# The end of a pipelined attention kernel: one DMA step, four high-part steps of ScalarE and a stretch of VectorE's order moved

## The chip, the cores and the metric

One core of one Trainium2 chip. The metric is the device time of one launch in microseconds (us); lower is better.

## What is computed

Two residual layers on x of shape (8, 1024, 512), conditioned on a vector of 256 per batch:

```python
# style = s @ aff_w.T + aff_b; every weight matrix is scaled by style per input and by rsqrt(sum of squares) per output
x = x + clip(modulated_linear(x, L0), -256, 256)
kx = modulated_linear(x, K).reshape(B, N, 16, 32)          # q = k = v = kx
scores = einsum('bnhd,bnjd->bnhj', kx, kx) / sqrt(32)      # 16 x 16 between the heads of one token
out = einsum('bnhj,bnjd->bnhd', softmax(scores), kx)
x = x + modulated_linear(out.reshape(B, N, 512), O)
```

## The kernel before, in words

All is float32 and held transposed: 512 features in four blocks of 128 partitions, tokens in the free dimension. The 8192 tokens are cut into 32 tiles of 256, numbered 0 to 31; `last` is 31. Each of the three linear layers L0, K, O takes four blocks per tile (`linear`, L446), and a block is twelve matmuls of 128x256: four input blocks by three passes. To keep float32 precision, operands are split in a high part, made by ScalarE (`hi_part`, L561: `x_hi_of`, `x1_hi_of`, `y_hi_of`), and a low part, made by VectorE (`lo_part`, L755). In the names of the trace the operand of L0 and of K is x_hi/x_lo and that of O is y_hi/y_lo. "O(29)" below is the O layer of tile 29, its four blocks.

What happens to one tile c, in order:

- L0: TensorE, evacuated from PSUM by ScalarE (`l0_out`), clipped and added to x by VectorE (`make_x1`, L839 and L841).
- K: four blocks, evacuated by ScalarE (`k_out`, trace kx<-lin_ps). The result goes to DRAM (`k_to_dram`, or block by block near the end, `k_blocks_to_dram` L263) and back in another layout (`k_from_dram` L272, four reads into k_st). VectorE turns it (`turn_k` L816, k_rhs<-k_st). This is "the turn of the keys".
- The keys are copied into a block diagonal tile k_bd, three quarters by GpSimd (`spread_k` L429), one by ScalarE (`copy_keys` L669). Then TensorE computes the scores (`scores`, L516, 64 small matmuls).
- Scores are merged from PSUM: the even ones by ScalarE (`even_scores` L633), the odd ones by VectorE (`merge_scores` L846), then maxima and subtraction (`subtract_maxima` L851, L853), the exponential on ScalarE (L655), `sums` (L865, L867), `normalise` (L871 and the transpose L877, which makes p_turned), and masks that spread the probabilities into p_bd: four on VectorE (`spread_probabilities` L884), four on ScalarE (`spread_some` L661).
- v takes its own way through DRAM: k_rhs written (`v_to_dram` L280), four reads into k_v (`v_from_dram` L288), two transposes by VectorE (`turn_v` L831).
- The product of probabilities and v (`pv`, L534, 64 small matmuls) is evacuated by ScalarE in two halves (`evacuate_y` L640, into the single buffer y), written to DRAM in four transfers (`y_to_dram` L296) and read back as one (`y_from_dram` L305, into the single buffer yr). Tile 31 has half of its writes issued by ScalarE (L649) and is read in two halves into a buffer of kx (L312).
- O: high and low parts of yr, four blocks, evacuated (`o_out`), added by VectorE (`finish` L860) and stored (`store` L319).

TensorE's program is a list of stages (L200 to L215). ScalarE, VectorE and SP each have their own list: a head, a regular pattern per loop index, and a tail that is written out by hand (`act_tail` L724, `dve_tail` L913, SP's L379 to L413). Nothing reorders these lists at run time: an engine, and SP's queue of transfers, does its steps in the order in which they stand, each waiting on its semaphores. All transfers but two at the end are issued by SP.

The waits that matter below:

- `evacuate_y(c, 0)` waits until the writes of c - 1 have landed, since y is a single buffer, and for pv(c).
- `v_from_dram(c)` waits for `turn_v(c - 1)`, since k_v is a single buffer.
- `y_from_dram(c)` waits for the landed writes of c and for high and low parts of c - 1, since yr is a single buffer.
- `y_hi_of(c)` waits for the landed read, `y_lo_of(c)` for the high parts.
- `scores(c)` waits for the copies of GpSimd and ScalarE, and for the merge of c - 1; `even_scores(c)` waits for scores(c).
- `pv(c)` waits for all eight masks of c, for `turn_v(c)` and for the evacuation of c - 1.

At the end TensorE's order is: K(30), pv(28), scores(29), K(31), two blocks of O(26), scores(30), two blocks of O(26), pv(29), one block of O(27), scores(31), three blocks of O(27), pv(30), O(28), pv(31), O(29), O(30), O(31).

Of the kernel before, what the change touches and what calls it, by code (L numbers as in the profile page):

```python
# [34 lines left out]
def build(nc, xT, condT, wT, affT, aff_b, lin_b, block_ones, token_mask, head_diag, dim_eye, outT):  # L35
# [32 lines left out]
    with ExitStack() as ctx:  # L68
# [126 lines left out]
        last = N - 1  # L195
# [35 lines left out]
        def _(sp):  # L231
# [44 lines left out]
            def v_to_dram(c):  # L276
                sp.wait_ge(v_krhs, c + 1)
                if c >= 2:
                    sp.wait_ge(v_in_landed, DMA * CT * (c - 1))
                sp.dma_start(v_dram[c % 2], k_rhs[:, :, :].rearrange("p w n -> p (w n)")).then_inc(v_out_landed, DMA)  # L280

            def v_from_dram(c):
                sp.wait_ge(v_out_landed, DMA * (c + 1))
                if c:
                    sp.wait_ge(v_v, c)
                src = v_dram[c % 2].rearrange("(r d) (c s) -> d r c s", d=HD, c=CT)
                for ct in range(CT):
                    sp.dma_start(k_v[HD * ct:HD * (ct + 1)].rearrange("p r x n -> p r (x n)"),  # L288
                                 src[:, :, ct]).then_inc(v_in_landed, DMA)

            def y_to_dram(c, js=range(HR)):
                sp.wait_ge(a_y, 2 * (c + 1))
                if c >= 2:
                    sp.wait_ge(y_in_landed, DMA * (c - 1))
                for j in js:
                    sp.dma_start(y_dram[c % 2].rearrange("(n d) t -> d n t", d=HD)[:, :, j * TB:(j + 1) * TB],  # L296
                                 y_sb[HD * j:HD * (j + 1), :, :, :].rearrange("p n l s -> p n (l s)")
                                 ).then_inc(y_out_landed, DMA)

            def y_from_dram(c):  # L300
                sp.wait_ge(y_out_landed, DMA * HR * (c + 1))
                if c:
                    sp.wait_ge(a_yhi, 2 * c)
                    sp.wait_ge(v_ylo, 2 * c)
                sp.dma_start(yr_sb[:], y_dram[c % 2].rearrange("(k p) t -> p k t", p=P)).then_inc(y_in_landed, DMA)  # L305
# [88 lines left out]
            v_from_dram(last - 1)  # L394
            v_to_dram(last)
            y_from_dram(last - 3)
            v_from_dram(last)
            y_to_dram(last - 2)
            y_from_dram(last - 2)
            y_to_dram(last - 1)  # L400
            y_from_dram(last - 1)
# [143 lines left out]
        def _(act):  # L545
# [143 lines left out]
            def act_steps(i):  # L689
# [37 lines left out]
                (last - 1, l0_out, 3), (last - 1, x1_hi_of, 1), (last, l0_out, 0), (last, l0_out, 1),  # L727
                (last, l0_out, 2), (last - 3, spread_some, 0), (last, l0_out, 3), (last - 3, spread_some, 1),
                (last - 3, spread_some, 2), (last - 3, spread_some, 3), (last - 1, k_out, 0), (last, x1_hi_of, 0),
                (last - 1, k_out, 1), (last - 2, copy_keys), (last - 1, k_out, 2), (last - 4, y_hi_of, 0),  # L730
                (last - 4, y_hi_of, 1), (last - 1, k_out, 3), (last, x1_hi_of, 1), (last - 3, evacuate_y, 0),
                (last - 3, evacuate_y, 1), (last - 2, even_scores), (last, k_out, 0), (last, k_out, 1),
                (last - 2, exponentials), (last, k_out, 2), (last, k_out, 3), (last - 1, copy_keys),
                (last - 5, o_out, 0), (last - 2, spread_some, 0), (last - 2, spread_some, 1),
                (last - 2, spread_some, 2), (last - 1, even_scores), (last - 2, spread_some, 3), (last - 5, o_out, 1),
# [18 lines left out]
        def _(dve):  # L754
# [133 lines left out]
            def dve_steps(i):  # L888
# [26 lines left out]
                (last - 1, make_x1, 0), (last - 3, sums), (last - 1, make_x1, 1), (last - 1, x1_lo_of, 0),  # L915
                (last - 1, x1_lo_of, 1), (last - 3, normalise), (last - 3, spread_probabilities), (last, make_x1, 0),
                (last - 2, turn_k), (last - 3, turn_v), (last, make_x1, 1), (last, x1_lo_of, 0), (last, x1_lo_of, 1),
                (last - 4, y_lo_of, 0), (last - 4, y_lo_of, 1), (last - 2, merge_scores), (last - 2, subtract_maxima),
                (last - 2, sums), (last - 1, turn_k), (last - 2, turn_v), (last - 2, normalise),
                (last - 2, spread_probabilities), (last - 1, merge_scores), (last - 1, subtract_maxima),  # L920
                (last, turn_k), (last, copy_last_keys), (last - 1, sums), (last - 1, normalise),
                (last - 1, spread_probabilities), (last, merge_scores), (last, subtract_maxima), (last - 1, turn_v),
# [47 lines left out]
```

## Time and profile before

| | us |
|---|---|
| three runs | 703.6, 705.45, 703.8 |
| median | 703.8 |
| the profiled execution, its own time | 701.4 |
| its span, from first to last instruction | 699.4 |
| TensorE busy | 684.7 |
| VectorE busy | 580.0 |
| ScalarE busy | 546.1 |
| GpSimd busy | 114.7 |

The mean granted TensorE clock of the profiled execution is 0.997 of full speed. The rows of the trace below count time from the start of the span. In them PE is TensorE, PEld its weight loads, DVE is VectorE, ACT is ScalarE, POOL is GpSimd, and SPq is SP's queue of DMA issues. A matmul's row gives its start and its length; matmuls overlap, so the distance between two starts is the time that one takes of the engine.

### The profile page before, as it was taken

The page shows a single profiled execution, that of the slowest core. Times are in us where ns is not written, and L with a number is a line of the kernel's source. Part 1 is how long each engine was busy: PE and PEld are TensorE (multiplying, and loading weights), DVE is VectorE, ACT ScalarE, POOL GpSimd, SP SyncE. Part 2 cuts the span into 40 slices and gives each one's busy share as a digit, 9 for nine tenths or more (in the row PEclk, how much of TensorE's full clock was granted, in tenths as well). Part 3 has the DMA queues.
Part 4 walks back from the last instruction along what each step waited for, and adds up shares of the span by engine and source line. Part 5 has one row for each costly group of instructions (what it writes and reads, how often), then busy time and mean ns, then how long its engine had stood idle before and what let it go on. Part 6 is the DMA issues. An engine that isn't in the chain of part 4 may idle for free.

```text
span 699.4 us, 21684 instructions
## 1 busy us (share of the span) xinstructions
PE 684.7 (98%) x8904; PEld 668.3 (96%) x8904; DVE 580.0 (83%) x1049; ACT 546.1 (78%) x1073; POOL 114.7 (16%) x105
## 2 busy tenths in 40 slices
PE   9999999999999999999999989999999999999987
PEld 8999999999999999999999989999999999998887
DVE  4689987889888899888889878899888899888854
ACT  6898977888777888777878777888777888777854
POOL 2022311111101111101111101111101111103100
PEclk9999999999999999999999999999999999999999
DMA  9467878577877677877768777778777678876666
GB/s 289 135 176 199 222 192 240 152 213 212 211 183 197 198 211 212 234 181 196 202 190 218 191 196 185 211 207 212 184 208 201 190 216 212 210 185 208 156 174 217
DMA packets 229794, 140.37 MB, mean 201 GB/s; under 512 B 141376, under 2 KB 223296, under 8 KB 229696
## 3 DMA queue, kind: packets, MB, share of 16 engines
q1 hardware_dynamic: 228640, 138.74, 73.3%
q8 instruction: 70, 1.15, 0.7%
q10 hardware_dynamic: 1056, 0.26, 0.2%
q14 instruction: 28, 0.23, 0.1%
HBM read 71.85 MB, written 67.11 MB: 199 GB/s over the span
## 4 chain that ended last, share of the span: by engine, by line
PE 37%; ACT 23%; DMA 14%; DVE 13%; SPq 6%; issue 6%; POOL 1%; ACTq 0%; DVEq 0%; POOLq 0%
PE lin_ps L464 28%; DMA yr<-y_turned 5%; DMA y_turned<-y 4%; ACT kx L558 4%; ACT p_bd L661 4%; ACT y_hi L567 4%; PE s_ps L516 3%; DMA k_turned<-kx 3%; ACT x_hi L567 3%; PE y_ps L534 3%; DVE x L841 2%; ACT o L558 2%; SPq L288 2%; SPq L272 2%; SPq L296 2%
## 5 line engine op out<-in xcount | busy, mean ns | idle before, releaser
L464 PE MATMUL lin_ps<-x_hi,w_hi 128*128 128x256 f32 x1024 | 290.1, 284 | 0.2
L464 PE MATMUL lin_ps<-x_hi,w_lo 128*128 128x256 f32 x1024 | 284.9, 279 | 0.7 <-issue 0.7
L464 PE MATMUL lin_ps<-x_lo,w_hi 128*128 128x256 f32 x1024 | 285.2, 279 | 0.0
L464 PEld LDWEIGHTS lin_ps<-x_hi,w_hi 128*128 128x128 f32 x1024 | 192.1, 188 | 9.1 <-issue 5.2
L429 POOL COPY k_bd<-k_rhs 32x1024 f32<-32x1024 f32 x94 | 110.3, 1174 | 540.8 <-DVE k_rhs L816 537.2
L464 PEld LDWEIGHTS lin_ps<-x_lo,w_hi 128*128 128x128 f32 x1024 | 192.2, 188 | 0.0
L464 PEld LDWEIGHTS lin_ps<-x_hi,w_lo 128*128 128x128 f32 x1024 | 192.2, 188 | 0.0
L567 ACT ACTIVATE x_hi<-x,style 128x256 fp32r<-128x256 f32 x256 | 114.9, 502 | 58.3 <-DVE x L841 51.9
L760 DVE SCALAR_TENSOR_TENSOR x_lo<-x,style,x_hi 128x256 fp32r<-128x256 f32 x256 | 147.5, 627 | 14.7 <-ACT x_hi L567 14.7
L464 PE MATMUL lin_ps<-y_hi,w_hi 128*128 128x256 f32 x512 | 145.1, 283 | 0.5 <-DVE y_lo L760 0.5
L464 PE MATMUL lin_ps<-y_lo,w_hi 128*128 128x256 f32 x512 | 144.2, 282 | 0.0
L464 PE MATMUL lin_ps<-y_hi,w_lo 128*128 128x256 f32 x512 | 144.2, 282 | 0.0
L464 PEld LDWEIGHTS lin_ps<-y_hi,w_hi 128*128 128x128 f32 x512 | 97.2, 190 | 1.9 <-issue 1.8
L464 PEld LDWEIGHTS lin_ps<-y_lo,w_hi 128*128 128x128 f32 x512 | 97.2, 190 | 0.0
L464 PEld LDWEIGHTS lin_ps<-y_hi,w_lo 128*128 128x128 f32 x512 | 97.2, 190 | 0.0
L661 ACT ACTIVATE p_bd<-p_turned,tok_mask 128x512 f32<-128x512 f32 x128 | 90.2, 715 | 5.3 <-DVE p_turned L877 5.2
L558 ACT ACTIVATE x<-lin_ps,bias,demod 128x256 f32<-128x256 f32 x136 | 72.6, 556 | 17.4 <-PE lin_ps L464 15.3
L558 ACT ACTIVATE kx<-lin_ps,bias,demod 128x256 f32<-128x256 f32 x128 | 68.4, 557 | 6.7 <-PE lin_ps L464 5.9
L558 ACT ACTIVATE o<-lin_ps,bias,demod 128x256 f32<-128x256 f32 x120 | 65.5, 555 | 10.4 <-PE lin_ps L464 10.0
L516 PE MATMUL s_ps<-k_bd,k_rhs 128*32 128x128 f32 x2048 | 62.4, 273 | 5.3 <-POOL k_bd L429 3.1
L534 PE MATMUL y_ps<-p_bd,v 128*32 128x128 f32 x2048 | 63.3, 276 | 2.8 <-ACT p_bd L661 2.6
L516 PEld LDWEIGHTS s_ps<-k_bd,k_rhs 128*32 128x32 f32 x2048 | 56.1, 110 | 6.9 <-POOL k_bd L429 3.5
(63 smaller groups left out, 726.3 us busy)
## 6 DMA issues: line engine op xcount, KB each, us to landing
k_st<-k_turned SPq DMA_DIRECT2D x128, 128.0 KB, 3.1
v_turned<-k_rhs SPq DMA_DIRECT2D x32, 512.0 KB, 6.0
k_v<-v_turned SPq DMA_DIRECT2D x128, 128.0 KB, 3.6
y_turned<-y SPq DMA_DIRECT2D x126, 128.0 KB, 3.4
x<-xT SPq DMA_DIRECT2D x31, 512.0 KB, 5.8
yr<-y_turned SPq DMA_DIRECT2D x31, 512.0 KB, 4.6
k_turned<-kx SPq DMA_DIRECT2D x30, 512.0 KB, 2.9
outT<-o SPq DMA_DIRECT2D x29, 512.0 KB, 4.3
```

What stands on the lines that cost most here:

```text
L272: sp.dma_start(k_st[HD * r:HD * (r + 1)], k_dram[c % 2].rearrange("(n d) t -> d n t", d=HD)[:, :, t0:t0 + TB]).then_inc(k_in_landed, DMA)
L288: sp.dma_start(k_v[HD * ct:HD * (ct + 1)].rearrange("p r x n -> p r (x n)"), src[:, :, ct]).then_inc(v_in_landed, DMA)
L296: sp.dma_start(y_dram[c % 2].rearrange("(n d) t -> d n t", d=HD)[:, :, j * TB:(j + 1) * TB], y_sb[HD * j:HD * (j + 1), :, :, :].rearrange( ...
L429: pool.tensor_copy(k_bd[HD * r:HD * (r + 1), r], k_rhs[HD * r:HD * (r + 1)]).then_inc(g_kbd, 1)
L464: mm = pe.matmul(lin_ps[:, (n + j) % NLB, 0:T], w[:, k, (m + j) * P:(m + j + 1) * P], r[:, k, :], start=(q == 0), stop=(q == len(passes) - 1))
L516: mm = pe.matmul(s_ps[HD * ct:HD * (ct + 1), x, q * P:(q + 1) * P], k_rhs[:, w:w + 2].rearrange("p w n -> p (w n)"), k_bd[:, :, w:w + 2].r ...
L534: mm = pe.matmul(y_ps[HD * j:HD * (j + 1), q // PB, (q % PB) * P:(q % PB + 1) * P], v_sb[:, c % 2, j * QS + q], p_bd[:, grp].rearrange("p ...
L558: act.activation(out, src, ACT.Identity, bias=bias_sb[l][:, m:m + 1], scale=demod[l][:, m, b:b + 1]).then_inc(a_lin, 1)
L567: a = act.activation(out[:, k], src[:, k], ACT.Copy, scale=style[l][:, k, b:b + 1])
L661: act.activation(p_bd[:, :, TG // 2 + t, :], p_turned[:], ACT.Copy, scale=tok_mask[:, TG // 2 + t:TG // 2 + t + 1]).then_inc(a_pbd, 1)
L760: v = dve.scalar_tensor_tensor(out=out[:, k], in0=src[:, k], scalar=style[l][:, k, b:b + 1], in1=hi[:, k], op0=ALU.mult, op1=ALU.subtract)
L841: dve.tensor_tensor(x1h, x1h, x_sb[:, c % 2, h * half:(h + 1) * half], ALU.add).then_inc(v_x1, 1)
```

## The change

Three edits, all in the hand-written end. Nothing is added or taken out; TensorE's and GpSimd's orders are as before.

1. SP: the four writes of the results of tile 29 come ahead of the four v reads of tile 31.
2. ScalarE: the high parts of 27 (`last - 4`) come behind the even scores of 29, so that all of K(30) is evacuated ahead of them; the key copy of 29 stands one evacuation later.
3. VectorE: the merge and the maxima of 29 come ahead of the low parts of 27; the turn of 30's keys comes ahead of the sums of 29, and v of 29 is transposed behind its normalising.

```diff
@@ SP
             v_to_dram(last)
             y_from_dram(last - 3)
+            y_to_dram(last - 2)
             v_from_dram(last)
-            y_to_dram(last - 2)
             y_from_dram(last - 2)
@@ act_tail
-                (last - 1, k_out, 1), (last - 2, copy_keys), (last - 1, k_out, 2), (last - 4, y_hi_of, 0),
-                (last - 4, y_hi_of, 1), (last - 1, k_out, 3), (last, x1_hi_of, 1), (last - 3, evacuate_y, 0),
-                (last - 3, evacuate_y, 1), (last - 2, even_scores), (last, k_out, 0), (last, k_out, 1),
+                (last - 1, k_out, 1), (last - 1, k_out, 2), (last - 2, copy_keys), (last - 1, k_out, 3),
+                (last, x1_hi_of, 1), (last - 3, evacuate_y, 0), (last - 3, evacuate_y, 1), (last - 2, even_scores),
+                (last - 4, y_hi_of, 0), (last - 4, y_hi_of, 1), (last, k_out, 0), (last, k_out, 1),
@@ dve_tail
-                (last - 4, y_lo_of, 0), (last - 4, y_lo_of, 1), (last - 2, merge_scores), (last - 2, subtract_maxima),
-                (last - 2, sums), (last - 1, turn_k), (last - 2, turn_v), (last - 2, normalise),
+                (last - 2, merge_scores), (last - 2, subtract_maxima), (last - 4, y_lo_of, 0), (last - 4, y_lo_of, 1),
+                (last - 1, turn_k), (last - 2, sums), (last - 2, normalise), (last - 2, turn_v),
```

SP's issues at the end, from the write of v of 31 on (v_turned and k_v belong to v, y_turned to the results; x4 are four transfers). Before:

```order
L280 DMA v_turned<-k_rhs 128x1024
L305 DMA yr<-y_turned 128x4x256
L288 DMA k_v<-v_turned 32x4x256 x4
L296 DMA y_turned<-y 32x16x64 x4
L305 DMA yr<-y_turned 128x4x256
```

Now:

```order
L280 DMA v_turned<-k_rhs 128x1024
L305 DMA yr<-y_turned 128x4x256
L296 DMA y_turned<-y 32x16x64 x4
L288 DMA k_v<-v_turned 32x4x256 x4
L305 DMA yr<-y_turned 128x4x256
```

The writes of 29 stand ahead of the v reads of 31; the reads of 28 and 29 keep their places around the two.

ScalarE (ACT) from the key copy of 29 (k_bd) on; kx are the evacuations of K, the first two blocks 2 and 3 of tile 30, the pair behind them blocks of tile 31. Before:

```order
L669 ACTIVATE k_bd<-k_rhs 32x1024
L558 ACTIVATE kx<-lin_ps,bias,demod 128x256
L567 ACTIVATE y_hi<-yr,style 128x256 x4
L558 ACTIVATE kx<-lin_ps,bias,demod 128x256
L567 ACTIVATE x_hi<-x,style 128x256 x2
L640 ACTIVATE y<-y_ps 128x16x32 x2
L633 ACTIVATE sc<-s_ps,odd_mask 128x512
L558 ACTIVATE kx<-lin_ps,bias,demod 128x256 x2
```

Now (block 2 of tile 30 stands ahead of the first row, so the first kx here is its block 3):

```order
L669 ACTIVATE k_bd<-k_rhs 32x1024
L558 ACTIVATE kx<-lin_ps,bias,demod 128x256
L567 ACTIVATE x_hi<-x,style 128x256 x2
L640 ACTIVATE y<-y_ps 128x16x32 x2
L633 ACTIVATE sc<-s_ps,odd_mask 128x512
L567 ACTIVATE y_hi<-yr,style 128x256 x4
L558 ACTIVATE kx<-lin_ps,bias,demod 128x256 x2
```

The four high parts moved from ahead of block 3 to behind the even scores.

VectorE (DVE) from the maxima of 29 to its masks (mx, sc, total, rcp, p_turned and p_bd belong to the softmax, k_rhs<-k_st is the turn of 30's keys, v<-k_v the transposes of 29). Before, with the low parts of 27 further ahead:

```order
L851 TENSOR_REDUCE mx<-sc 128x32
L853 TENSOR_TENSOR sc<-sc,mx 128x512
L865 TENSOR_REDUCE total<-sc 128x32
L867 RECIPROCAL rcp<-total 128x32
L816 COPY k_rhs<-k_st 128x1024
L831 STREAM_TRANSPOSE v<-k_v 128x512 x2
L871 TENSOR_TENSOR sc<-sc,rcp 128x512
L877 STREAM_TRANSPOSE p_turned<-sc 128x512
L884 TENSOR_SCALAR p_bd<-p_turned,tok_mask 128x32x16 x4
```

Now:

```order
L851 TENSOR_REDUCE mx<-sc 128x32
L853 TENSOR_TENSOR sc<-sc,mx 128x512
L760 SCALAR_TENSOR_TENSOR y_lo<-yr,style,y_hi 128x256 x4
L816 COPY k_rhs<-k_st 128x1024
L865 TENSOR_REDUCE total<-sc 128x32
L867 RECIPROCAL rcp<-total 128x32
L871 TENSOR_TENSOR sc<-sc,rcp 128x512
L877 STREAM_TRANSPOSE p_turned<-sc 128x512
L831 STREAM_TRANSPOSE v<-k_v 128x512 x2
L884 TENSOR_SCALAR p_bd<-p_turned,tok_mask 128x32x16 x4
```

The low parts of 27 now stand between the subtraction of 29 and the turn of 30's keys, and four steps of 29's softmax behind that turn.

## Rows read from the trace of the kernel before

**Rows 1.** The page, busy us, share of the span and instructions.

```profile
PE 684.7 (98%) x8904; PEld 668.3 (96%) x8904; DVE 580.0 (83%) x1049; ACT 546.1 (78%) x1073; POOL 114.7 (16%) x105
```

**Rows 2.** Waits of PE, 628 to 700 us: total us, times, longest.

```profile
PE s_ps L516 <- POOL k_bd L429: 3.1, 2, 2.6
PE y_ps L534 <- ACT p_bd L661: 2.6, 1, 2.6
PE lin_ps L464 <- DVE y_lo L760: 0.5, 1, 0.5
```

**Rows 3.** Stretches: length, busy PE, PEld, DVE, ACT, POOL, PEclk, DMA share, GB/s.

```profile
648.00:650.00 2.00, 1.61 (x60) 1.62 (x64) 1.95 (x5) 1.69 (x3) 0.33 (x1) 1.00 1.13 215
...
676.00:678.00 2.00, 2.00 (x19) 1.61 (x11) 2.00 (x6) 2.00 (x5) 0.00 (x0) 0.50 0.00 0
```

**Rows 4.** The chain that ended last, from 600 us: start, us, what.

```profile
636.01 1.69 DMA k_turned<-kx
...
643.60 1.11 DVE k_rhs L816
...
646.95 1.40 POOL k_bd L429
...
653.35 1.89 PE y_ps L534 x64
...
666.66 3.52 DMA y_turned<-y
...
677.29 4.40 DMA yr<-y_turned
...
683.68 11.69 PE lin_ps L464 x96
```

**Rows 5.** Timeline of ACT: start, us, instruction, idle before and its releaser.

```profile
632.29 1.05 ACT L669 ACTIVATE k_bd<-k_rhs 32x1024 f32<-32x1024 f32 x1
...
635.43 0.55 ACT L558 ACTIVATE kx<-lin_ps,bias,demod 128x256 f32<-128x256 f32 x1
...
656.69 1.09 ACT L640 ACTIVATE y<-y_ps 128x512 f32<-128x512 f32 x2
...
670.20 1.09 ACT L640 ACTIVATE y<-y_ps 128x512 f32<-128x512 f32 x2 [4.71 <-DMA y_turned<-y]
```

**Rows 6.** Timelines of POOL (first row) and DVE.

```profile
644.76 3.57 POOL L429 COPY k_bd<-k_rhs 32x1024 f32<-32x1024 f32 x3 [9.59 <-DVE k_rhs L816]
...
661.88 1.30 DVE L831 STREAM_TRANSPOSE v<-k_v 128x512 f32<-128x512 f32 x2
...
675.53 1.68 DVE L760 SCALAR_TENSOR_TENSOR y_lo<-yr,style,y_hi 128x256 fp32r<-128x256 f32 x4 [5.32 <-ACT y_hi L567]
```

**Rows 7.** Timeline of PE: scores of 30, product of 31, two matmuls of O(29).

```profile
648.39 1.84 PE L516 MATMUL s_ps<-k_bd,k_rhs 128*32 128x128 f32 x60 [2.55 <-POOL k_bd L429]
...
673.82 2.83 PE L534 MATMUL y_ps<-p_bd,v 128*32 128x128 f32 x64 [2.61 <-ACT p_bd L661]
676.58 0.58 PE L464 MATMUL lin_ps<-y_hi,w_hi 128*128 128x256 f32 x1
...
678.03 0.34 PE L464 MATMUL lin_ps<-y_hi,w_hi 128*128 128x256 f32 x1
```

**Rows 8.** Timeline of SP's queue: start of the first issue, us of all.

```profile
654.92 0.60 SPq L305 DMA_DIRECT2D yr<-y_turned  x1
663.25 1.74 SPq L288 DMA_DIRECT2D k_v<-v_turned  x4
665.09 3.03 SPq L296 DMA_DIRECT2D y_turned<-y  x4
...
678.19 1.86 SPq L296 DMA_DIRECT2D y_turned<-y  x2
...
683.42 1.51 SPq L312 DMA_DIRECT2D kx<-y_turned  x2
```

**Rows 9.** The line L305, 31 reads of the results: us from issue to landing.

```profile
DMA to landing us min/median/max: 4.0/4.6/5.8
```

## Prediction

> **What bounds the kernel now.** I read the page first, for the engines: TensorE is busy 98% of the span [rows 1]. In the loop a change of order can win nothing, the time is TensorE's work. So the next question is where TensorE stands still in the tail. The view of its waits from 628 us on says: 3.1 us before scores (two waits, the longer 2.6), 2.6 before a product with v, 0.5 before an output block [rows 2], together 6.2 us. The stretches show that the second hole costs more than its wait: after it the granted clock is 0.50, the lower level of 1.2 GHz, while after the equal hole at 645.8 it stayed at 1.00 [rows 3]. The product of tile 31 takes 2.83 us at the lower clock where the same 64 matmuls took 1.89 for tile 29, and six spacings of the linear matmuls behind it take 1.45 us where the last 96 matmuls of the kernel stand 0.122 apart (11.69/96), which makes 0.73 [rows 4, 7]. So the clock costs 0.94 + 0.72 = 1.7 us, and the second hole 4.3 in all.
>
> The chain that ended last says who ends the waits.
>
> *First hole.* ACT makes the high parts of 27, only then evacuates K's last block of 30, done at 635.98 [rows 5]; 1.69 us to land in DRAM; four reads; the turn by DVE 643.60 to 644.71 [rows 4]; three POOL copies to 648.33 [rows 6]; scores of 30 at 648.39.
>
> *Second hole.* DVE transposes v of 30 (to 663.18) [rows 6]; SP issues the four v reads of 31 that waited for it [rows 8]; behind them in the same queue the four writes of 29's results from 665.09, landed at 670.18 [rows 4, 8]; only then may ACT evacuate 30's results (its row has 4.71 us idle on that DMA) [rows 5]; the masks of 31; the product of 31 at 673.82 [rows 7].
>
> **The change part by part.** It adds and removes no instruction. Three moves.
>
> *ACT, the high parts of 27.* In the new order block 2 of K(30), the key copy of 29 and block 3 run back to back from 632.29: 0.55 + 1.05 + 0.55 with small gaps, so block 3 is done at 634.5 in place of 635.98 [rows 5]: **1.5 us earlier.** What is pushed back: the key copy of 29 now ends at 633.9, under POOL's copies for 29, which release those scores alone in rows 2 (0.5 us), so at no cost. The high parts of 27 now stand behind the scores of 29 and their even part and run from 638.0 to 639.7. K(31)'s first evacuation slips by 0.8 us, covered: SP comes to that block only after the v reads of 29, and TensorE needs its PSUM bank again only four blocks later.
>
> *DVE, the key turn of 30.* Merging, maxima and subtracting of 29 now come first and end at 640.3, the low parts of 27 follow (1.66 us, 1.68 for those of 29 [rows 6]) to 641.9. The keys of 30 land 1.5 us earlier than now (643.60 to 642.1 [rows 4]), so DVE is free 0.2 us before they come, and turns them 642.1 to 643.2. Sums, reciprocal, normalising and turn of 29 now stand behind this and still end by 645.9, v of 29 is transposed by 647.2, its masks done by 648.9, and its product is due at 651.7: covered.
>
> POOL copies from 643.25 for 3.57 us as now [rows 6], to 646.85. TensorE is ready at 645.8 (648.39 less its wait of 2.55 [rows 7]), so **the first hole shrinks from 2.6 to 1.0 us: 1.5 won.** Above, the three copies take 3.3 if the third is no longer than its fellows: 1.8 won. Below: the third copy took 1.40 while DVE normalised [rows 4], some 0.35 more than the others, and the new order puts this normalising (644.25 to 644.95) onto the second copy. If it holds POOL up there by its whole 0.7 us, 1.2 is won. I take 1.5, since the group as a whole pays the same disturbance now.
>
> The Trainium skill, "SBUF — State Buffer", section "Who interferes with whom", speaks against this move: a DVE instruction with two SBUF inputs and a GpSimd instruction that reads SBUF shut each other out for the whole instruction. By it the first win is the 1.2 and the whole change 4.4.
>
> The 1.5 us travel on, because each next step waits for this chain: scores of 30 end at 648.85, keys of 31 are turned from 651.9 behind the maxima of 30, scores of 31 start at 655.5, v of 30 is transposed by 661.7 (663.18 now [rows 6]) and releases pv(30) at 661.95.
>
> *SP, the writes of 29.* These results are evacuated 656.69 to 657.78 [rows 5], by the shift until 656.3. SP has issued nothing between the read of 28 at 654.92 and the v reads at 663.25 [rows 8]. Now the writes go at 656.35 to 658.9 and land 5.1 us after the first issue (665.09 to 670.18), 6 if crowded: 661.5 to 662.5. The four v reads of 31 that they are moved past wait in both orders for the transpose that ends at 661.7; they lose nothing as long as the results are evacuated by 659. The read of 29 follows at 663.6 (now 670.2), landed by 668.2 at its median of 4.6 [rows 9].
>
> ACT's evacuation of 30 then has only pv(30) (done 663.85) and its own queue in front: 664.1 to 665.2, **six us earlier**. What is late next: the probabilities of 31 are turned at 665.85, the masks take under 3 us, v of 31 is transposed by 668.8. TensorE ended O(28) at 671.2 (673.82 less 2.61 [rows 7]); 1.45 earlier, and with 0.3 that I allow for changing over, pv(31) starts at 670.05: all its inputs are there, **3.8 won, and 0.94 more since the clock does not fall.** It ends at 671.95 and O(29) starts at 672.0 in place of 676.58. The high parts of 29 run on ACT behind the masks and two evacuations until 671.1, the low ones until 671.95 (677.21 now [rows 6]): 5.25 earlier.
>
> From there the stage runs as now, shifted. The read of 30 waits for those low parts, and O(30) started 6.4 us after its issue (677.29 to 683.68) [rows 4]: 678.4. TensorE needs 6.64 − 0.72 for O(29) (676.58 to 683.68 less the wait of 0.46) and is done at 677.9, so a wait of 0.5 stands here, as now. The results of 31 are evacuated behind pv(31) 5.0 earlier, written from 673.2 and landed 5.2 later (678.19 to 683.42) [rows 8]: 678.45. Read back in the 4.4 of the read of 30, plus the 2.0 from landing to first matmul (681.69 to 683.68) [rows 4]: O(31) at 684.85, after a wait of 0.6. Now it starts at 683.68 + 5.85 = 689.55. **The sum is 689.55 − 684.85 = 4.7 us**, about 1.3 of it from the keys of 30 and 3.4 from the results of 29. Behind O(31) nothing changes. The span goes from 699.4 to 694.7, the profiled time from 701.4 to 696.7. The median of the runs is 703.8, 2.4 above the profiled time, and I take the sum off the median: **699.1**.
>
> Bounds: 5.5 if O(31) follows the low parts of 29 by the shift of 5.25 and POOL is quick; 3.3 if the read of 30 or of 31 takes the longest landing of its group, 5.8, in place of 4.4 [rows 9].
>
> **The rivals.**
>
> 1. *The key chain does not move*, because DVE comes late to the keys (parts of 27 and the scores of 29 now stand in front, margin 0.2 us) or POOL is held up. The first hole stays; only the results of 29 count, 3.4: 700.4. For: the margin, and a chain of scores, even part, high parts and low parts now ends in the turn. Against: to eat all of it takes 1.7 us of lateness.
> 2. *The wait moves instead of going.* All results pass DRAM through one buffer yr; DMA engines are at shares of 1.13 in one of the stretches [rows 3]. If both last reads land in 5.8, O(30) and O(31) each wait 1.4 more: 4.7 − 2.8 = 1.9: 701.9. For: no slack, there is a wait of 0.5 already. Against: the pattern behind the low parts of 29 is today's.
> 3. *Slower: the lower clock catches the last stages.* Per matmul it costs 0.12 more (1.45/6 less 0.122). It fell after a hole of 2.6 us, and the waits before O(30) and O(31) could come to that by rival 2. If it stays down for all of both, 96 × 0.12 = 11.5 us: 703.8 − 4.7 + 11.5 = 710.6. It decides from (4.7 + 2.1)/0.12 = 57 slow linear matmuls on. Against: it was down for seven of them, and the hole at 645.8 lowered nothing.
> 4. *The writes of 29 go no earlier*, their evacuation waiting for something else. Then 1.5 are left: 702.3. Against: it ended at 657.78, and only the v transpose released SP at 663.25.
>
> **How the numbers follow.** Forecast 0.62; rival 1, 0.18; rivals 2 and 4 together 0.16, of which 0.06 still gain more than 2.1 us; rival 3, 0.04. "Same" is within 0.3%, 2.1 us, about what a measurement of this kernel can tell. Faster 0.62 + 0.18 + 0.06 = 0.86, same 0.10, slower 0.04. The range goes from 697.6 (the 5.5, and 0.7 for a median of three runs that spread over 1.8) to 702.0 (rival 2).
>
> **What would show it.** K's last evacuation of 30 ends near 634.5, the turn of its keys starts near 642.1, TensorE waits about 1 us for POOL before scores(30). The writes of 29 start near 656.4, and ACT's evacuation of 30 is not idle on a DMA. pv(31) follows O(28) within 0.4 us and takes 1.9, no stretch has a clock under 0.9, and waits of about half a us stand before O(30) and O(31). I am wrong if the turn of 30's keys starts at 643.6 or later, or if one of the last two stages waits over 2.5 us.

## The result

The changed kernel takes 700.08 us (median of 10 executions, 695.48 to 701.78) against 704.68 for the kernel before on the same chip (10, 701.09 to 709.39): 4.6 us less. The ratio is 0.9905, 95% interval 0.9876 to 0.9934. A second measurement on another occasion gave 699.31 (10) against 704.65 (33), ratio 0.9911 [0.9883, 0.9939]. The forecast was 699.1 us and a gain of 4.7, which is a ratio of 0.9933 and so lies just inside the interval, at its small end.

The profiled execution of the changed kernel took 701.17 us, with a span of 699.1, only 0.3 less than the span of before. It is the second slowest of its ten (spans 693.7 to 699.7), so its trace shows what worked and also what can go wrong. I use it with the profiled execution of the second measurement, 697.78 us, span 694.7.

The page, as in [rows 1]: nothing has changed in the amount of work.

```profile
PE 684.5 (98%) x8904; PEld 668.3 (96%) x8904; DVE 579.8 (83%) x1049; ACT 546.4 (78%) x1073; POOL 114.7 (16%) x105
```

The waits of TensorE (PE) in the tail of the changed kernel (total us, times, longest), which answer to [rows 2]:

```profile
PE s_ps L516 <- POOL k_bd L429: 2.9, 2, 2.4
PE lin_ps L464 <- DVE y_lo L760: 2.3, 1, 2.3
PE y_ps L534 <- DVE v L831: 0.7, 1, 0.7
```

The wait for ACT's masks before the product of 31 (2.6 us) is gone. The wait before the scores of 30 is 2.4 instead of 2.6, where 1.0 was forecast. A wait of 2.3 us stands before O(30), where 0.5 was forecast. The 0.7 us in the last row stand before the product of 28, ahead of everything that the edits move.

ACT and SP in the timeline of the changed kernel, as in [rows 5, 8]:

```profile
634.52 0.57 ACT L558 ACTIVATE kx<-lin_ps,bias,demod 128x256 f32<-128x256 f32 x1
...
666.02 1.09 ACT L640 ACTIVATE y<-y_ps 128x512 f32<-128x512 f32 x2
```

```profile
658.33 2.88 SPq L296 DMA_DIRECT2D y_turned<-y  x4
663.77 1.73 SPq L288 DMA_DIRECT2D k_v<-v_turned  x4
665.61 0.38 SPq L305 DMA_DIRECT2D yr<-y_turned  x1
```

The writes of 29 start at 658.33 instead of 665.09, and ACT's evacuation of 30 at 666.02 has no idle time in front of it, where it had 4.71 us on the transfer. The first row is K's last evacuation of 30, done at 635.1. This execution runs 0.7 us late from the loop on (the turn of 29's keys starts at 630.89, before at 630.20), so against the loop that evacuation is 1.6 us earlier, as forecast.

The chain of waits of the changed kernel, as in [rows 4]:

```profile
635.11 2.93 DMA k_turned<-kx
...
644.06 1.11 DVE k_rhs L816
...
646.31 1.45 POOL k_bd L429
...
673.91 5.91 DMA yr<-y_turned
...
681.81 13.27 PE lin_ps L464 x96
```

Three rows matter. K's last write took 2.93 us where it took 1.69. The read of 30's results took 5.91 where it took 4.40. And the last 96 matmuls took 13.27 us where they took 11.69: the clock fell there. The stretches of the same execution (length, busy us of the five engines, PEclk, DMA share, GB/s) say the same, as [rows 3] did for the hole of before:

```profile
672.00:674.00 2.00, 2.00 (x67) 1.80 (x56) 1.86 (x5) 2.00 (x6) 0.00 (x0) 1.00 0.00 0
674.00:676.00 2.00, 2.00 (x20) 2.00 (x19) 2.00 (x4) 0.90 (x2) 0.00 (x0) 1.00 0.37 80
682.00:684.00 2.00, 2.00 (x12) 2.00 (x12) 2.00 (x5) 0.46 (x2) 0.00 (x0) 0.59 0.84 277
684.00:686.00 2.00, 2.00 (x12) 2.00 (x11) 0.27 (x1) 0.57 (x1) 0.00 (x0) 0.55 1.02 350
```

The product of 31 (671.73 to 673.69) now runs at the full clock, and the low clock has moved to the start of O(30).

The other execution of the same kernel, in its chain of waits:

```profile
634.59 2.56 DMA k_turned<-kx
...
642.73 1.11 DVE k_rhs L816
...
672.54 4.33 DMA yr<-y_turned
...
678.86 11.85 PE lin_ps L464 x96
```

Here the transfers are shorter, the wait before O(30) is 0.7 us and the clock stays up.

### The profile page after: what moved, and what is told of

Read it like the earlier page. It is cut to its first block, busy times and chain, and to the rows that moved or that the text cites. A ratio compares the mean times of both kernels' runs of the same rounds, so it can differ in the third digit from the quotient of the medians.

```text
span 699.1 us, 21684 instructions
## 1 busy us (share of the span) xinstructions
PE 684.5 (98%) x8904; PEld 668.3 (96%) x8904; DVE 579.8 (83%) x1049; ACT 546.4 (78%) x1073; POOL 114.7 (16%) x105
## 4 chain that ended last, share of the span: by engine, by line
PE 85%; ACT 4%; DMA 4%; DVE 4%; issue 2%; SPq 1%; POOL 1%; ACTq 0%; DVEq 0%; POOLq 0%
PE lin_ps L464 68%; PE s_ps L516 7%; PE y_ps L534 7%; DMA yr<-y_turned 2%; PE s_ps L474 1%; ACT p_bd L661 1%; DMA k_turned<-kx 1%; ACT kx L558 1%; DMA k_st<-k_turned 1%; DVE y_lo L760 1%; ACT x_hi L567 1%; POOL k_bd L429 1%; DMA y_turned<-y 1%; ACT y_hi L567 0%; PE y_ps L497 0%
## 5 line engine op out<-in xcount | busy, mean ns | idle before, releaser
L760 DVE SCALAR_TENSOR_TENSOR x_lo<-x,style,x_hi 128x256 fp32r<-128x256 f32 x256 | 147.3, 627 | 13.4 <-ACT x_hi L567 13.4
L558 ACT ACTIVATE o<-lin_ps,bias,demod 128x256 f32<-128x256 f32 x120 | 65.5, 555 | 13.1 <-PE lin_ps L464 12.9
```

What stands on the lines that cost most here:

```text
L558: act.activation(out, src, ACT.Identity, bias=bias_sb[l][:, m:m + 1], scale=demod[l][:, m, b:b + 1]).then_inc(a_lin, 1)
L760: v = dve.scalar_tensor_tensor(out=out[:, k], in0=src[:, k], scalar=style[l][:, k, b:b + 1], in1=hi[:, k], op0=ALU.mult, op1=ALU.subtract)
```

## The experiments

Each was measured beside the kernel before. The last column but one is a length read from each trace, from the turn of 29's keys (the last step that no edit touches) to the end of the span. It leaves out what happens in the loop. The clock's share of the time can be estimated from the mean granted clock of each execution: one minus that clock, times the span, is about what the lower clock costs.

| kernel | ratio to before, 95% | median us (executions) | turn of 29's keys to turn of 30's | wait before scores of 30 / those scores | wait before product of 31 / that product | wait before O(30) | tail | mean granted clock 0.999 or more |
|---|---|---|---|---|---|---|---|---|
| before | 1 | 703.8 to 704.67 (92) | 13.4 | 2.55 / 1.95 | 2.61 / 2.83 | 0.5 | 69.2 | 1 of 92 |
| changed | 0.9905 | 700.08 (10) | 13.2 | 2.41 / 1.96 | none / 1.96 | 2.3 | 68.2 | 5 of 10 |
| after_again | 0.9911 | 699.31 (10) | 12.4 | 1.57 / 1.95 | none / 1.95 | 0.7 | 64.3 | 5 of 10 |
| sp_only | 0.9938 [0.9911, 0.9965] | 701.15 (12) | 13.3 | 2.42 / 3.58 | none / 1.96 | 1.2 | 67.2 | 3 of 12 |
| act_dve_only | 0.998 [0.9952, 1.0008] | 703.38 (12) | 13.2 | 2.40 / 3.52 | 2.55 / 3.46 | 0.9 | 70.8 | 1 of 12 |
| act_only | 1.0001 [0.997, 1.0032] | 706.06 (12) | 14.1 | 3.62 / 3.42 | 3.33 / 3.3 | 1.2 | 73.0 | 0 of 12 |
| dve_only | 1.0009 [0.9986, 1.0032] | 704.64 (12) | 13.8 | 3.0 / 3.27 | 3.31 / 3.2 | 1.5 | 72.2 | 0 of 12 |
| before_filler | 0.998 [0.9958, 1.0002] | 702.76 (12) | 12.9 | filled / 1.96 | filled, 0.99 left / 1.95 | 0.8 (0.8 and 0.2 before O(29) and O(31)) | 69.9 | 7 of 12 |
| filler | 0.9935 [0.991, 0.9961] | 698.34 (12) | 13.2 | filled / 1.95 | none / 1.96 | filled (1.0 before O(31)) | 66.9 | 10 of 12 |
| v_write_later | 0.994 [0.9912, 0.9969] | 699.08 (12) | 12.4 | 1.64 / 1.95 | none / 1.95 | 2.5 | 66.2 | 5 of 12 |
| own_buffer | 0.9915 [0.9886, 0.9945] | 697.75 (11) | 13.1 | 2.37 / 3.52 | none / 1.96 | none (0.6 before O(31)) | 66.4 | 6 of 11 |
| own_buffer_v_later | 0.9917 [0.9885, 0.9949] | 696.70 (12) | 12.3 | 1.44 / 1.95 | none / 1.95 | 1.0 (0.2 before O(31)) | 64.8 | 7 of 12 |
| own_buffer_filler | 0.9876 [0.9846, 0.9906] | 695.62 (6) | 11.9 | filled / 1.96 | none / 1.95 | filled | 63.4 | 5 of 6 |
| all_filler | 0.9922 [0.9896, 0.9949] | 698.88 (8) | 12.8 | 1.1 behind 8 fillers / 1.95 | none / 1.95 | filled (0.6 before O(31)) | 65.0 | 3 of 8 |

The last column counts executions whose clock, averaged over the whole span, rounds to 0.999 or 1.0, that is, those in which it practically never fell. It does not say where in the span the clock fell.

**The SP move alone** (sp_only):

```diff
             y_from_dram(last - 3)
+            y_to_dram(last - 2)
             v_from_dram(last)
-            y_to_dram(last - 2)
```

> Only the writes of 29 go ahead of the v reads of 31; ACT and DVE as before. Theory A (the prediction's sum: 3.4 us from the results of 29, 1.3 from the keys of 30): 3.4 us faster than before, ratio 0.995, 1.3 us slower than the whole change. Theory B (read from the changed kernel's trace: the keys landed only 0.2 us earlier against the loop because their last write took 2.93 us instead of 1.69, so the two other moves bring nothing): as fast as the whole change within 0.5 us. In the trace both want the writes of 29 near 658, no idle time of ACT on a transfer before it evacuates 30, and product of 31 within 0.5 us of O(28)'s end.

0.9938 is 4.4 us, more than the 3.4 of theory A and less than the whole change by 2 us, but the intervals overlap. Theory B, that this move is everything, wanted both equal within 0.5 us; the times lean to A and do not rule B out. Its trace has the writes of 29 early and no wait before the product of 31. It has also something that the kernel before did not show in its profile, in the chain of waits:

```profile
649.65 3.58 PE s_ps L516 x64
...
676.24 4.75 DMA yr<-y_turned
...
682.98 11.73 PE lin_ps L464 x96
```

The scores of 30 took 3.58 us and not 1.95, behind a wait of 2.42 us: the clock fell at the first hole.

**The moves on ACT and DVE alone** (act_dve_only): the other two parts of the diff.

> Only the moves on ACT and DVE; SP as before, so the writes of 29 wait behind the v reads of 31. Theory A: 1.3 to 1.5 us faster than before, ratio 0.998, scores of 30 released 1.5 us earlier against the loop. Theory B: within 0.5 us of before, the turn of 30's keys at most 0.3 us earlier against the loop, and a last K write of 30 that takes about 2.9 us. Both: the 2.6 us hole before the product of 31 and the low clock behind it stay.

0.998, 1.4 us faster, which is what theory A wanted, but the interval holds no change as well. The turn of the keys was only 0.2 us earlier against the loop, and K's last write of 30 took 3.00 us, both as theory B wanted. So neither theory is borne out fully: the time fits A, this one trace fits B. ACT's evacuation of 30 stands as it did before the change, idle on the transfer:

```profile
673.29 1.09 ACT L640 ACTIVATE y<-y_ps 128x512 f32<-128x512 f32 x2 [4.66 <-DMA y_turned<-y]
```

**ACT's move alone, DVE's move alone** (act_only, dve_only): each one of the two lists as changed, the other as before.

> ACT's move alone (high parts of 27 behind the even scores of 29), DVE's order as before: the low parts of 27 still stand ahead of the merge of 29, and now wait for high parts that end only near 639.7. Worked out on the trace before: low parts end 640.5, merge, maxima and subtraction 642.7, exponential 643.4, sums and reciprocal 644.4, turn of 30's keys 644.45 instead of 643.60. Theory A and B alike: slower than before by 0.5 to 1.0 us (ratio 1.001), the turn of 30's keys released by DVE's own work and not by the transfer. If it is as fast as before, DVE's move was not needed.

Forecast 14.25 us from turn to turn (644.45 instead of 643.60, so 13.4 + 0.85), measured 14.1. The mechanism is in DVE's timeline: the low parts wait 2.19 us for ScalarE's high parts, no row waits for a transfer, and the turn follows DVE's own work.

```profile
639.38 1.68 DVE L760 SCALAR_TENSOR_TENSOR y_lo<-yr,style,y_hi 128x256 fp32r<-128x256 f32 x4 [2.19 <-ACT y_hi L567]
640.97 0.75 DVE L846 SCALAR_TENSOR_TENSOR sc<-s_ps,odd_mask,sc 128x512 f32<-128x512 f32 x1
...
643.86 0.69 DVE L865 TENSOR_REDUCE total<-sc 128x32 f32<-128x512 f32 x1 [0.70 <-ACT sc L655]
...
644.86 1.00 DVE L816 COPY k_rhs<-k_st 128x1024 f32<-128x1024 f32 x1
```

The median is 1.4 us above that of before, the ratio of 1.0001 does not tell it from no change.

> DVE's move alone; ACT still makes the high parts of 27 before K's last block of 30. Theory A: the keys of 30 land when they did, the turn follows that of 29 by 13.4 us as before, nothing is gained before the scores of 30; within 0.5 us of before, ratio 0.999 to 1.001. If it gains 1 us or more, the key part of the change did not need ACT's move.

Ratio 1.0009, no gain, as expected. Taken singly neither move gains. The design needs both, since ACT's is to bring the keys earlier and DVE's to turn them when they come; that the pair gains time is not shown, its interval holds no change.

**The whole change again** (after_again).

> The whole change once more on the same chip as the three others. Theory A and B: 4 to 5 us faster than before, ratio 0.993 to 0.995. Its executions lay in two groups so far, spans of 693.7 to 695.3 and of 697.7 to 699.7; if the lower clock behind the wait before O(30) makes the upper group, a profile of the lower group shows no stretch under 0.9 there and the last 96 matmuls in about 11.7 us instead of 13.27.

It was measured at 0.9911, more than the 4 to 5 us expected. Its profiled execution has what was described for the lower group: no fall of the clock, the last 96 matmuls in 11.85 us. The turn of the keys is 1.0 us earlier against the loop. The two groups themselves did not come again: the ten spans go from 694.7 to 699.5 without a gap like the one of the first ten.

**Fillers** (filler): unread matmuls that keep TensorE at work in the holes.

```diff
+            def fill(c, n):
+                pe.wait_ge(v_sc, c + 1)
+                for _ in range(n):
+                    pe.matmul(s_ps[:, 0, 0:P], w_hi[L0][:, 0, 0:P], w_hi[L0][:, 0, 0:P], start=True, stop=True)
...
-            + blocks(K, last) + blocks(O, last - 5, [0, 1]) + one("scores", last - 1) + blocks(O, last - 5, [2, 3])
+            + blocks(K, last) + blocks(O, last - 5, [0, 1]) + [("fill", last - 2, 28)]
+            + one("scores", last - 1) + blocks(O, last - 5, [2, 3])
...
-            + one("pv", last - 1) + blocks(O, last - 3) + one("pv", last) + blocks(O, last - 2) + blocks(O, last - 1)
+            + one("pv", last - 1) + blocks(O, last - 3) + one("pv", last) + blocks(O, last - 2) + [("fill", last, 10)]
+            + blocks(O, last - 1)
```

> The whole change, and 28 matmuls on constant weights ahead of the scores of 30 and 10 ahead of O(30), whose results nobody reads (28 x 128 columns are about 1.6 us, in a hole of 1.6 to 2.4). Theory C: a hole of about 2.4 us before a stage makes the granted clock fall in some executions and not in others, and that costs 1.6 us each time (scores of 30 took 3.5 us instead of 1.95 in three of the last four profiles, O(30) and O(31) together 13.27 instead of 11.7 in one). Then the upper group of the executions disappears: median 1 to 2 us below that of the whole change (ratio to before 0.987 to 0.990), highest run below 699, scores of 30 in 1.95. Theory D: the spread comes from the loop or from the transfers and not from the clock; then the fillers change nothing or cost up to 0.5 us, ratio 0.991 to 0.992, same spread of 6 us.

The clock did what theory C said: it stayed up in 10 of 12 executions against 10 of 20 of the change without fillers. The ratio of 0.9935 is no better than the change's, and the highest execution was 701.09. The chain shows where a part of the clock's gain went:

```profile
646.55 3.08 PE s_ps L482 x28
```

The 28 matmuls took 3.08 us, not 1.6, and held TensorE 0.7 us beyond a hole of 2.4. The rest of the loss is not explained.

**Fillers in the kernel before** (before_filler): the same function, 18 ahead of the scores of 30 and 18 ahead of the product of 31, all else as before the change.

> The kernel before, with 18 unread matmuls ahead of the scores of 30 and 18 ahead of the product of 31 (28 of them took 3.08 us, so 18 take 2.0, a bit less than the holes of 2.55 and 2.61); order of all else as before. It takes the clock out and leaves the order. Theory C (the low clock behind the holes costs 1.6 to 1.7 us each time, always behind the second hole, in part of the executions behind the first): mean granted clock 0.999 or more in most executions (0 of 67 executions of the kernel before have that), 2 to 3 us faster than before, ratio 0.996 to 0.997, and still 2 us slower than the whole change. Theory D (the fall of the clock is not tied to these two holes): within 0.7 us of before.

The clock stayed up in 7 of 12 executions, against 1 of 92, so most of the falls are tied to these holes. The scores of 30 took 1.96 us in the profile and the product of 31 1.95. The gain was 1.4 us, with an interval from 0 to 3, less than the 2 to 3 expected. The whole change, whose clock cost as much (1.2 us on average by the estimate above), is 4.9 us better than this by the ratios, 2.7 to 3.4 by the medians, measured on different occasions: that much is the order and not the clock.

**K's writes ahead of v's** (v_write_later), on top of the change:

```diff
-            k_blocks_to_dram(last - 1, [0])
-            v_to_dram(last - 2)
-            k_blocks_to_dram(last - 1, range(1, KB))
+            k_blocks_to_dram(last - 1, range(KB))
+            v_to_dram(last - 2)
```

> The whole change, and SP writes the four K blocks of 30 ahead of the write of v of 29, which they share the DMA engines with. Theory E: K's last write of 30 takes 2.6 to 3.0 us instead of 1.69 in the changed kernel because it now overlaps the 512 KB write of v. Then it takes 1.7 to 2.0 here and the turn of 30's keys follows that of 29 by 11.6 to 12.2 us (13.17 and 12.36 in two profiles of the whole change, 13.40 before); 0.5 to 1.0 us faster than the whole change, ratio 0.989 to 0.991. Rival F: the slow write comes from K's own four blocks, now sent within 2.4 us instead of 4; then it stays at 2.6 or more, and v, written later, may delay the turn further (it waits for that write too): ratio 0.991 to 0.993.

From its chain of waits:

```profile
633.28 2.05 DMA k_turned<-kx
...
671.25 6.14 DMA yr<-y_turned
```

K's last write took 2.05 us, and 2.10 and 2.21 in the two later kernels with this order, against 2.33 to 3.00 in five traces of the change's order of transfers. The landing says it more clearly: SP issues the first read of 30's keys, which waits for all of K's writes, 6.3 to 6.4 us after the turn of 29's keys in the three traces with v later, 6.6 to 7.2 in the seven with ScalarE's new order and v's write first, and 7.5 in the four with ScalarE's old order. That is theory E's direction and a part of its size; K's own four blocks, closer together now, are not the only cause (rival F wanted 2.6 or more); whether they make the rest was not tried. Turn to turn is 12.4, 12.3 and 12.8 us, not 11.6, since the reads behind it took from 5.4 to 6.4 us in the traces where the turn waited for them. No time was won (0.994): the read of 30's results took 6.14 us here, and a wait of 2.5 us stood before O(30).

**A buffer of its own for the results of 30** (own_buffer), on top of the change:

```diff
-            return yr_sb if c < N - 1 else yr_last
+            return yr_sb if c < N - 2 else kx_sb[:, 1] if c == N - 2 else yr_last
...
-                if c:
+                if c == last - 1:
+                    sp.wait_ge(k_out_landed, DMA * k_transfers(last))
+                elif c:
                     sp.wait_ge(a_yhi, 2 * c)
                     sp.wait_ge(v_ylo, 2 * c)
-                sp.dma_start(yr_sb[:], y_dram[c % 2].rearrange("(k p) t -> p k t", p=P)).then_inc(y_in_landed, DMA)
+                sp.dma_start(results_of(c)[:], y_dram[c % 2].rearrange("(k p) t -> p k t", p=P)).then_inc(y_in_landed, DMA)
```

> The whole change, and the results of 30 are read back into the second buffer of kx, so that this read waits for its writes alone and no longer for high and low parts of 29. Theory G: the wait before O(30) (2.3 and 0.7 us in two profiles) is ended by the round trip of 30 through DRAM, whose read starts only behind the low parts of 29, so the read starts up to 1 us earlier and the wait ends as much earlier, and with it the fall of the clock there: 0.5 to 1.5 us faster than the whole change, ratio 0.989 to 0.991. Rival: the writes of 30 land no earlier than those low parts are done (issue of the last one 670.1 plus 3.5 is 673.6, read issued 673.9): within 0.3 us of the whole change.

```profile
672.86 0.38 SPq L307 DMA_DIRECT2D kx<-y_turned  x1
```

The read starts at 672.86 and the low parts of 29 end at 673.86, so it started 1.0 us sooner than it could have. In this trace O(30) does not wait; a wait of 0.6 us stands before O(31). The median is 2.3 us below the changed kernel's, but measured on another occasion, and the ratio 0.9915 is the same as the change's. So the earlier read of theory G is shown in the trace, not in the time, and the next limit is near: with the same buffer in the next kernel O(30) waited 1.0 us, on ScalarE. Ahead of the high parts it issued two of tile 31's writes, from 671.38 for 2.64 us, and evacuated two blocks; it was never idle on the read.

**Both** (own_buffer_v_later):

> Both of the last two edits together. If both act and are independent, their gains add: 1 to 2.5 us faster than the whole change, ratio 0.987 to 0.990. If only one acts, as fast as that one.

0.9917: the median is the lowest of these four, 696.70, and the spread the widest, up to 702.69. No addition is shown.

**Own buffer and short fillers** (own_buffer_filler): 10 ahead of the scores of 30 and 5 ahead of O(30).

> The whole change with its own buffer for the results of 30 and shorter fillers than in the first attempt: 10 ahead of the scores of 30 (1.1 us in a hole of 1.6 to 2.4), 5 ahead of O(30) (0.55 us). Theory C: the first fillers won the clock but overran the hole (3.08 us in 2.4) and paid with time; these don't, so 1 to 1.5 us faster than own_buffer alone and below the change and before: ratio 0.986 to 0.990. If the fillers cost in other ways (each one is a weight load and a matmul on the path), ratio 0.991 or more.

Ratio 0.9876 [0.9846, 0.9906], the best of all, 695.62 us and 9 below the kernel before. From its chain of waits:

```profile
646.69 1.96 PE s_ps L526 x64
...
677.80 11.46 PE lin_ps L468 x96
```

No wait is left before O(30) and O(31). It has only six executions, it is the best of the twelve runs here, and its interval still overlaps that of the change.

**All together** (all_filler): own_buffer_v_later with 8 and 5 fillers.

> Everything together: the whole change, K's writes of 30 ahead of v's of 29, own buffer for the results of 30, 8 fillers ahead of the scores of 30 and 5 ahead of O(30). If the gains add: 0.5 to 1 us below own_buffer_filler, ratio 0.985 to 0.989; if the earlier keys only move the wait to later stages, the same as own_buffer_filler.

0.9922, worse than expected by more than the interval. The profiled execution is the slowest of its eight, and its tail, 65.0 us long, does not explain it: the turn of 29's keys started at 636.57, 6.4 us later than in the kernel before. The time went in the loop. The view of TensorE's waits from 20 to 625 us gives:

```profile
PE s_ps L525 <- issue: 2.1, 1, 2.1
PE lin_ps L467 <- issue: 1.7, 1, 1.7
```

The clock fell behind each of the two (the same columns as in [rows 3]):

```profile
408.00:410.00 2.00, 2.00 (x12) 2.00 (x13) 1.20 (x2) 0.69 (x1) 0.00 (x0) 0.66 0.37 123
...
538.00:540.00 2.00, 2.00 (x12) 2.00 (x12) 1.62 (x3) 0.34 (x2) 0.00 (x0) 0.59 0.64 214
```

An estimate from the granted clock of these stretches and the next ones puts the two falls at 3.4 us together. The waits are 3.8 us against 2.9 in the kernel before, so falls and waits make more than four of the 6.4 us. Such "issue" waits, which have no releaser in the profile, add up to between 0 and 3.8 us in the loops of the fourteen traces. Apart from some under 0.3 us they keep to two places, near 406 us in ten traces and near 533 in eight, with 0.5 to 2.7 us each. Only here did the clock fall behind them; waits of 2.15, 2.46 and 2.73 us at the first place and of 1.79 and 1.80 at the second left it at full in other traces. What causes them stays open, and with them whether this combination is worse.

## Why the prediction was right, and where its steps were off

*The total.* Forecast 4.7 us; the medians give 4.6 and 5.3, the ratios 6.7 and 6.3, with intervals that go down to 4.7 and 4.3. Right in size, and rather too small than too large. A part of that is luck, as the next points show: the keys came less early than forecast in both traces, and the clock's share came out right through other falls than the forecast's. The prediction's own sign of being wrong, a turn of 30's keys at 643.6 or later, was met in the profiled execution (644.06) and not in the other (642.73), and the stretches at 0.59 and 0.55 break its "no stretch has a clock under 0.9".

*The writes of 29* (3.4 us). The mechanism is shown step by step: writes at 658.33 (forecast 656.35, plus 0.7 for this execution's loop and 1.3 for the key chain that did not come early), no idle time of ACT on the transfer, the product of 31 without a wait and in 1.96 us. Alone the move measured 4.4, interval 2.5 to 6.3. The 3.4 has the clock's 1.7 in it; in the trace of the move alone the product of 31 ran at the full clock, and the clock fell at the first hole.

*The key chain* (1.5 us at the scores of 30, 1.3 in the sum). Here a step was mis-sized. "1.5 us earlier" holds for the evacuation (1.6). "The keys of 30 land 1.5 us earlier" does not: they were turned 0.2 us earlier against the loop in one execution and 1.0 in the other. From turn to turn the six traces with both moves and the old order of K's and v's writes have 11.9 to 13.2 us, mean 12.8, and the four with ScalarE's old order 12.9 to 13.8, mean 13.35: some 0.5 us earlier on average, less than either group's own spread. I moved the landing by the shift of the evacuation and kept K's last write at 1.69 us, as if its neighbours in the queues would shift too. They don't: the 512 KB write of v of 29 still starts when it did, and K's four blocks now run close behind it. The write took 2.33 to 3.00 us, and the first read of the keys was issued 0.3 to 0.9 us earlier against the loop, not 1.5. The experiment that writes v later made that 1.1 to 1.2, so the overlap is a part of the reason; I left that collision out. DVE was free long before the keys came (1.55 us idle), so rival 1 came half true, but by the transfer and not by the DVE that I had put into it.

*POOL's copies.* 3.64 us for the three against 3.57, so taking the same value was right. The disturbance moved to the second copy, as said: 1.45 us while DVE normalised (646.18 to 646.87), the others 1.03 and 1.04. The price is 0.42 us, nearer to the 0.35 of before than to the whole 0.7. The Trainium skill, "SBUF — State Buffer", section "Who interferes with whom", has the right pair and the right direction. The whole 0.7, which the prediction read from it, did not come. The slow copy ends 0.9 us after the normalising, which is less than a whole copy of 1.03; so it had begun, or the record's start is early.

*The clock.* The step that failed is the reading of the first hole: "after the equal hole at 645.8 it stayed at 1.00", and in rival 3 "the hole at 645.8 lowered nothing". One trace cannot say that. Of seven profiles with a wait of 2.37 us or more before the scores of 30, five have those scores at 3.27 to 3.58 us, so the clock fell; two, the changed kernel and the one of before on which I built, do not. At the four waits of 1.64 and less there it did not. In the executions of before the mean granted clock is 0.996 or less in 59 of 92, where the profiled one had 0.997. So most executions of the kernel before pay for a fall that its profile did not show. That it stands at the first hole is likely, since sp_only, whose orders up to that hole are those of the kernel before, has a fall there; but a mean does not say where, and in all_filler two falls stood in the loop.

The clock does not explain why the ratios are on the large side of the forecast. By the estimate from the mean clock, the lower level costs 2.9 us on average in the 92 executions of before and 1.1 and 1.2 in the two times ten of the changed kernel: 1.8 us won, where the forecast had 1.7. That the two agree is luck: the forecast took the second fall away whole and knew of no first one, and the runs have more falls before the change and some left after it. The rest of the gain is the order, forecast at 3.0 us: 4.5 to 4.9 by the ratios, 2.8 to 3.5 by the medians, and the comparison with before_filler says the same. The writes of 29 alone gave 4.4 by the ratio and 3.5 by the medians, of which 1.0 is clock by the same estimate. Whether a step gives more than forecast stays open.

*The new wait.* Rival 2 and the start of rival 3 happened in the profiled execution: the read of 30 took 5.91 us, nearly the bound of 5.8, O(30) waited 2.3, and the clock fell for 1.6 us (13.27 less 11.69). In the other it took 4.33, the wait was 0.7, and the clock stayed up. The forecast had 0.5 here and took the 4.4 of one row, in a stage that it had itself called without slack. The mirror image of this is rival 3's price: the clock cost 1.6 us and not 11.5, since it came back within the stage.

## What to carry to other kernels

When a step is moved forward, go through every transfer on its path and ask what it will now overlap; moving a time by the shift of its releaser is only right if the neighbours shift too. Where TensorE waits some 2 us or more, the price has two values, with and without the fall of the clock, and one profile shows one of them; look at the granted clock of many executions before relying on either, and in a trace for where it fell. Filling such holes with unread matmuls held the clock here. With fillers longer than the hole it won no time; the kernel with short ones was the fastest, on six executions.

## What the runs showed of the hardware

- The length of TensorE's wait does not decide alone whether the clock falls. Holes of 2.55 and 2.41 us before the scores of 30 left it at full, holes of 2.42, 2.40 and 2.37 did not. At O(30) a wait of 2.3 us lowered it and one of 2.5 did not. In the loop waits of 2.11 and 1.72 us lowered it in one trace, and waits of 2.15, 2.46 and 2.73 did not in three others. By the granted clock of the stretches each fall cost 1.6 to 1.7 us.
- An unread fp32r matmul of 128x128x128 takes 0.11 us each in a row of 28 (3.08 us), at full clock.
- The same 512 KB read of the results of 30 took 4.33 to 6.14 us in eight traces (4.33, 4.40, 4.75, 4.82, 4.85, 5.07, 5.91, 6.14).
- The same 128 KB write of K's last block took 1.68 or 1.69 us in the four traces with ScalarE's old order, and 2.05 to 3.00 in eight where the blocks follow each other more closely.
